# Second layer of a two-layer gated cross-attention kernel: the query projection of groups 3 to 6 as seven block products

## The reference, cut to what matters

```python
def reference(x, ctx, ...):                       # x, ctx: 16 x 64 x 512, float32
    x = x + tanh(g_xattn[0]) * attention_0(layernorm(x), ctx)    # 32 heads of 128, 8 key heads, rotary, mask
    x = x + tanh(g_ffn[0])   * moe(layernorm(x))                 # 16 experts, 2 taken
    x = x + tanh(g_xattn[1]) * attention_1(layernorm(x), ctx)
    x = x + tanh(g_ffn[1])   * lora_moe(layernorm(x))            # 4 experts, 2 taken
    return x

def attention_1(h, ctx):
    q = (h @ Wq.T) -> 32 heads;  k, v = (ctx @ Wk.T), (ctx @ Wv.T) -> 8 heads, each for 4 query heads
    q, k = rmsnorm(q) * q_norm_w, rmsnorm(k) * k_norm_w
    return softmax(q @ k.T / sqrt(128)) @ v -> heads side by side @ Wo.T
```

## Time and profile before

| what | value |
|---|---|
| median of 3 runs | 1178.98 us (1178.72 to 1179.44) |
| profiled execution, its own time | 1179.01 us |
| its span | 1177.1 us |
| TensorE busy | 1169.5 us, 99% |
| VectorE busy | 880.9 us, 75% |
| GpSimd busy | 532.9 us, 45% |
| ScalarE busy | 424.0 us, 36% |
| steps 6 to 13 of layer 2 (866.10 to 1074.70) | 208.60 us |

### The profile page before, as it was taken

One profiled execution on the slowest core, in us unless ns is written; L12 is line 12 of the kernel. 1 busy time (PEld: TensorE's weight loads), 2 busy tenths in 40 slices (PEclk: granted clock), 3 DMA queues, 4 the chain that ended last, 5 costly groups with the idle time before them and its releaser, 6 DMA issues.

```text
span 1177.1 us, 17132 instructions
## 1 busy us (share of the span) xinstructions
PE 1169.5 (99%) x6272; PEld 946.7 (80%) x6272; DVE 880.9 (75%) x1538; ACT 424.0 (36%) x748; POOL 532.9 (45%) x371
## 2 busy tenths in 40 slices
...
PEclk9999999999999999999999999999999999999999
...
DMA packets 57315, 106.54 MB, mean 91 GB/s; under 512 B 3633, under 2 KB 36529, under 8 KB 51889
## 3 DMA queue, kind: packets, MB, share of 16 engines
...
## 4 chain that ended last, share of the span: by engine, by line
PE 96%; DVE 2%; issue 0%; ACT 0%; DVEq 0%; POOL 0%; POOLq 0%
PE ps_q L226 14%; PE ps_b L226 14%; PE ps_b L228 14%; PE ps_b L227 14%; PE ps_q L227 13%; PE ps_q L228 13%; PE ps_s L978 5%; PE ps_b L1005 4%; PE ps_s L278 1%; PE ps_q L953 1%; PE ps_q L2152 1%; PE ps_b L479 1%; PE ps_s L1847 1%; PE ps_q L529 0%; PE ps_b L529 0%
## 5 line engine op out<-in xcount | busy, mean ns | idle before, releaser
L226 PE MATMUL ps_q<-hT_hi,wq_hi 128*128 128x512 f32 x512 | 203.2, 397 | 0.0
L227 PE MATMUL ps_q<-hT_lo,wq_hi 128*128 128x512 f32 x512 | 199.6, 390 | 0.0
L228 PE MATMUL ps_q<-hT_hi,wq_lo 128*128 128x512 f32 x512 | 199.2, 389 | 0.0
L226 PE MATMUL ps_b<-wo_hi,o_hi 128*128 128x512 f32 x440 | 171.6, 390 | 0.0
L227 PE MATMUL ps_b<-wo_lo,o_hi 128*128 128x512 f32 x440 | 171.2, 389 | 0.0
L228 PE MATMUL ps_b<-wo_hi,o_lo 128*128 128x512 f32 x440 | 171.2, 389 | 0.0
L743 POOL TENSOR_TENSOR wq_lo<-wq_raw,wq_hi 128x512 fp32r<-128x512 f32 x64 | 90.2, 1413 | 112.8 <-ACT wq_hi L737 112.8
L1317 POOL TENSOR_TENSOR qT<-q_t 128x512 f32<-128x512 f32 x64 | 89.8, 1405 | 66.3 <-DVE q_t L1430 60.8
L226 PEld LDWEIGHTS ps_q<-hT_hi,wq_hi 128*128 128x128 f32 x512 | 96.1, 188 | 24.3 <-issue 1.5
L228 PEld LDWEIGHTS ps_q<-hT_hi,wq_lo 128*128 128x128 f32 x512 | 96.1, 188 | 20.3
L227 PEld LDWEIGHTS ps_q<-hT_lo,wq_hi 128*128 128x128 f32 x512 | 96.2, 188 | 18.7
...
## 6 DMA issues: line engine op xcount, KB each, us to landing
...
```

The costliest lines, as they stand in the source:

```text
L226: nc.tensor.matmul(dst, l_hi, r_hi, start=first, stop=False)
L227: nc.tensor.matmul(dst, l_hi, r_lo, start=False, stop=False)
L228: return nc.tensor.matmul(dst, l_lo, r_hi, start=False, stop=last)
```

## The change

The weights of a group (512 inputs by 4 heads of 128) and the tokens of a half (512 by 512) are each taken as 2 by 2 blocks. In groups 3 to 6 the four blocks of the query are built from seven products of blocks (Winograd's form) in place of eight. It needs sums of weight blocks (`s1` to `s4`, on GpSimd once a group) and sums of token blocks (`t1` to `t4`, made once for the layer), each split into a high and a low part. A product is 12 matmuls of 256 columns, so a unit has 84 in place of 48 of 512. The results are joined by five adds on VectorE out of PSUM into `qT`, and one copy on ScalarE. The unit's squares are then made from `qT` or the bank in four pieces, and folded by VectorE in two pieces of all four heads (`fold_woven`) in place of four.

The token sums are made with the tiles: ScalarE copies the front tiles' blocks out of the bank (`mixed_front`), VectorE makes t1 and t2 out of the later tiles' banks, GpSimd makes t3 and t4, and the splits follow in steps 2 to 5.

Other edits in layer 2: the eight small copies of the sums move from VectorE to ScalarE in all folded units; TensorE takes the sums of squares ahead of the scores, and waits for the folded squares before the last matmul of the output projection; values wait for the added outputs in two halves; the q and k norm weights are multiplied into the keys; the turned probabilities of units 3 to 13 go into `s_sb` in place of `pT`, which makes the next unit's turned scores wait for `p_lo`; groups 2 and 6 are written out beside the loop; a few semaphore increments are left out; SBUF regions are laid out anew.

```diff
+        def mixed_front(act, i):
+
+            c = lns[2]
+            own, bank = mixed_columns(i), ln_bank(c, i).rearrange("p (k t) -> p k t", k=KC)
+            act.wait_ge(*c("lo", i + 1))
+            nc.scalar.activation(b11_f[:, :, own], bank[:, 0:2, :], ACT.Copy)
+            nc.scalar.activation(b21_f[:, :, own], bank[:, 2:4, :], ACT.Copy).then_inc(att[1]["t_hi"], 1)
...
+            if c is lns[2] and i % PAIRS >= 2:
+                own, bank = mixed_columns(i), ln_bank(c, i).rearrange("p (k t) -> p k t", k=KC)
+                late = i // PAIRS * 2 + i % 2
+                dve.wait_ge(att[1]["t_hi"], late + 1)
+                nc.vector.tensor_tensor(t1_f[:, :, own], bank[:, 0:2, :], b11_f[:, :, own], ALU.subtract).then_inc(att[1]["t_f"], 1)
+                dve.wait_ge(att[1]["t_f"], 2 * late + 1)
+                nc.vector.tensor_tensor(t2_f[:, :, own], bank[:, 2:4, :], t1_f[:, :, own], ALU.subtract).then_inc(att[1]["t_f"], 1)
```

```diff
+        WOVEN_PARTS = ("a11", "s2", "s3", "a12", "s1", "a22", "s4")
...
+        def woven_low(pool, gt, name):
+
+            c = att[1]
+            pool.wait_ge(*c("woven_hi", 7 * (gt - W0) + WOVEN_PARTS.index(name) + 1))
+            f, hi, lo = woven_parts(name)
+            nc.gpsimd.tensor_tensor(lo, f, hi.bitcast(F32), ALU.subtract).then_inc(c["woven_lo"], 1)
+
+        def woven_first_sum(pool, gt):
+
+            s1_f = woven_parts("s1")[0]
+            pool.wait_ge(*att[1]("wq_in", 16 * (gt + 1)))
+            nc.gpsimd.tensor_tensor(s1_f, s1_f, woven_parts("a22")[0], ALU.add).then_inc(att[1]["s_f"], 1)
+
...
+        def woven_last_sum(pool, gt):
+
+            c = att[1]
+            if not (isinstance(gt, int) and gt == W0):
+                pool.wait_ge(*c("q_done", 8 * gt))
+            nc.gpsimd.tensor_tensor(s4_f[:, :, :], woven_parts("a12")[0], s2_f[:, :, :], ALU.subtract).then_inc(c["s_f"], 1)
```

```diff
+            def project_woven(g, h):
+
+                u = 2 * g + h
+                n = u - 2 * W0
+                left = {name: woven_parts(name)[1:] for name in WOVEN_PARTS}
+                tok = [slice(h * HALF + a * QT, h * HALF + (a + 1) * QT) for a in range(2)]
+                own = slice(h * QT, (h + 1) * QT)
+                tokens = lambda rows, a: (hT_hi[:, 2 * rows:2 * rows + 2, tok[a]], hT_lo[:, 2 * rows:2 * rows + 2, tok[a]])
+                mixed = lambda hi, lo: (hi[:, :, own], lo[:, :, own])
+
+                def product(bank, name, right, first, last_one=False):
+
+                    if h == 0:
+                        turn = 7 * (g - W0) + WOVEN_PARTS.index(name) + 1
+                        pe.wait_ge(*c("woven_hi", turn))
+                        pe.wait_ge(*c("woven_lo", turn))
+                    l_hi, l_lo = left[name]
+                    r_hi, r_lo = right
+                    for q in range(2):
+                        for k in range(2):
+                            col = slice(q * D, (q + 1) * D)
+                            dst, closes = bank[:, q * QT:(q + 1) * QT], last_one and (q, k) == (1, 1)
+                            nc.tensor.matmul(dst, l_hi[:, k, col], r_hi[:, k, :], start=first and (q, k) == (0, 0), stop=False, skip_group_check=True)
+                            nc.tensor.matmul(dst, l_hi[:, k, col], r_lo[:, k, :], start=False, stop=False, skip_group_check=True)
+                            last = nc.tensor.matmul(dst, l_lo[:, k, col], r_hi[:, k, :], start=False, stop=closes, skip_group_check=True)
+                    return last
+
+                pe.wait_ge(*c("ssq_t", u))
+                if h == 0:
+                    pe.wait_ge(*c("t_hi", 8))
+                    pe.wait_ge(*c("t_lo", 4))
+                product(ps_q[0], "a11", tokens(0, 0), True).then_inc(c["product"], 1)
+                product(ps_q[1], "s2", mixed(t2_hi, t2_lo), True, True).then_inc(c["product"], 1)
+                pe.wait_ge(*c("s_turned", u))
+                product(ps_h[0], "s3", mixed(t3_hi, t3_lo), True).then_inc(c["product"], 1)
+                pe.wait_ge(*c("copied", n + 1))
+                product(ps_q[0], "a12", tokens(1, 0), False, True).then_inc(c["q_done"], 1)
+                product(ps_h[1], "s1", mixed(t1_hi, t1_lo), True).then_inc(c["q_done"], 1)
+                pe.wait_ge(*c("joined", 5 * n + 2))
+                product(ps_h[0], "a22", mixed(t4_hi, t4_lo), False, True).then_inc(c["q_done"], 1)
+                pe.wait_ge(*c("joined", 5 * n + 3))
+                product(ps_h[1], "s4", tokens(1, 1), False, True).then_inc(c["q_done"], 1)
```

```diff
-                    pe.wait_ge(*c("q_fold", 4 * u + 4))
+                    folded_sums(u, h)
+                else:
+                    pe.wait_ge(*c("q_rot", 4 * u + 4))
...
+            def squares_ready(u):
+
+                pe.wait_ge(*c("q_rot", 4 * u + 4))
+                pe.wait_ge(*c("q_fold", 4 * u + 4))
...
+                    if ahead is not None and j == J - 1:
+                        squares_ready(ahead)
+                    last = nc.tensor.matmul(bank, o_lo[:, t, j, :], hi, start=False, stop=j == J - 1)
```

```diff
+            def fold_woven(u, r):
+
+                own, tok = fold_part(r)
+                other = fold_part(1 - r)[0]
+                dve.wait_ge(*c("q_sq", 4 * u + 2 * r + 2))
+                nc.vector.tensor_tensor(q_sq[own, :, tok], q_sq[own, :, tok], q_sq[other, :, tok], ALU.add).then_inc(c["q_fold"], 2)
```

```diff
+            def woven_step(g, h, next_wq):
+                u = 2 * g + h
+                n = u - 2 * W0
+                building = builds_woven(lay, g, next_wq)
+                if h == 0:
+                    for name in WOVEN_PARTS[4:]:
+                        woven_low(pool, g, name)
+                    for j in range(J):
+                        wo_low(g - 1, j)
+                elif building:
+                    woven_low(pool, g + 1, "a11")
+                att_shift(pool, lay, u - 1)
+                if h and building:
+                    woven_last_sum(pool, g + 1)
+                    woven_low(pool, g + 1, "s2")
+                elif next_wq:
+                    att_wq_low(pool, lay, g + 1, 0)
+                att_normalise(pool, lay, u - 1)
+                if h == 0 and not (isinstance(g, int) and g == G - 2):
+                    woven_first_sum(pool, g + 1)
+                    pool.wait_ge(*c("p_lo", u))
+                    woven_next_sums(pool, g + 1)
+                elif building:
+                    woven_low(pool, g + 1, "s3")
+                    pool.wait_ge(*c("p_lo", u))
+                    woven_low(pool, g + 1, "a12")
+                elif next_wq:
+                    for j in range(1, J):
+                        att_wq_low(pool, lay, g + 1, j)
```

```diff
+            def woven_step(g, h):
+                u, us, up = 2 * g + h, 2 * g + h - 1, 2 * g + h - 2
+                n = u - 2 * W0
+                heads = lambda bank: bank.rearrange("p (j t) -> p j t", j=2)
+                early, late = slice(0, QT), slice(QT, HALF)
+                part_b, part_d = qT[:, h, 0:2, late], qT[:, h, 2:4, late]
+
+                def joined(out, bank, part):
+                    return nc.vector.tensor_tensor(out, heads(bank), part, ALU.add)
+
+                turn_scores(us, 1 - h)
+                scale_scores(us)
+                dve.wait_ge(*c("copied", n + 1))
+                dve.wait_ge(*c("product", 3 * n + 2))
+                joined(part_b, ps_q[1], part_b).then_inc(c["joined"], 1)
+                att_mask(dve, lay, us, 1 - h)
+                dve.wait_ge(*c("joined", 5 * n + 1))
+                dve.wait_ge(*c("product", 3 * n + 3))
+                joined(part_d, ps_h[0], part_b).then_inc(c["joined"], 1)
+                maxima(us)
+                dve.wait_ge(*c("q_done", 4 * u + 2))
+                dve.wait_ge(*c("joined", 5 * n + 2))
+                joined(part_d, ps_h[1], part_d).then_inc(c["joined"], 1)
+                out_low(up, 0)
+                out_low(up, 1)
+                dve.wait_ge(*c("q_done", 4 * u + 3))
+                joined(qT[:, h, 2:4, early], ps_h[0], part_b).then_inc(c["joined"], 1)
+                out_low(up, 2)
+                dve.wait_ge(*c("q_done", 4 * u + 4))
+                joined(part_b, ps_h[1], part_b).then_inc(c["joined"], 1)
+                sums(us)
+                out_low(up, 3)
+                add_output(up, h, 0)
+                turn_probs(us)
+                fold_woven(u, 0)
+                fold_woven(u, 1)
+                att_probs_low(dve, lay, us)
+                add_output(up, h, 1)
+                add_output(up, h, 2)
+                if not (isinstance(g, int) and h):
+                    turn_sums(u, h)
+                add_output(up, h, 3)
```

317 lines of the change are left out of this document (270 added, 47 removed).

## The result

| | before | after |
|---|---|---|
| median, 8 runs each | 1179.20 us (1178.72 to 1179.69) | 1182.28 us (1180.41 to 1183.99, and one of 2347.24) |
| ratio | | 1.0025, 95% interval 1.0015 to 1.0035 |
| profiled execution, span | 1179.01, 1177.1 | 1180.41, 1178.5 |

One execution of the changed kernel took twice the time at a full granted clock; it is a disturbed run and is left out of the ratio. The change made the kernel a little slower: 3 us in the median, but only 1.4 us in the execution that was profiled, the fastest of the eight. Two executions take 1180.4 to 1180.5 with a mean granted clock of 1.000, the five others 1182.0 to 1184.0 with 0.999 to 0.996. A mean of 0.999 by itself says nothing: before's profiled execution has it too, because the clock is at 0.58 in its last 2.1 us (1175.0 to 1177.1), where TensorE has no work left.

The account below looks back on a forecast made before the run. TensorE, with work 99% of the span, was taken as the bound. Its gain of 6.9 us against +1.3 opening, +1.5 even steps, +2.9 step 6 and +0.9 steps 13 and 14 gave -0.3: 1178.7 us, range 1173.0 to 1183.6.

Parts of the forecast that it names:

- Step 6: t4_lo lengthens GpSimd's chain over mask and small maxima; s4 waits 2.8, restart 0.1: +2.9 us (0.5 to 4).
- TensorE's row: 84 matmuls of 256 columns at 0.119 us replace 48 of 512: 0.86 gained a unit, 6.9 over eight units.
- odd step: Steps 7, 9, 11: one GpSimd low, the mask keeps the port, cost 0; about 25.2 us from score to score.
- Rivals 2 and 5: 2: narrow matmuls at 0.106, 1174.7, chance 0.07; 5: they do not cover weight loads, +8.2 a unit, about 1244, chance 0.02.
- Even steps: Steps 8, 10, 12: eight GpSimd lows delay the mask and third add, s4 waits: 0.5 each, +1.5 us.
- P: Start of a step's first projection matmul, 870.18 in step 6, from which the working counts its times in us.
- Steps 13 and 14: VectorE's row longer by 1.2, TensorE's shorter by 0.9, values wait for added outputs: +0.9 us (0 to 1.5).
- The opening: Token sums stand in front of three TensorE waits, in expert network's tail, steps 0 and 2: +1.3 us (0.5 to 2.2).
- Rival 1: The lock costs nothing: VectorE gets the port first at mask and small maxima, s4 waits nowhere; 1174.3 us, chance 0.23.
- Rival 3: Slower: GpSimd gets the port at odd steps' mask and even steps' multiply; up to 1184.8, middle 1183, chance 0.18.
- Rival 4: VectorE's row is the bound, adds, mask and folds losing to GpSimd; gain gone, 1179 to 1182 us, chance 0.08.
- The copies: Eight copies of the sums leave VectorE's woven step, 1.43 us removed there; ScalarE takes them in 1.90.

Follow-up runs that it names:

- e1: The changed kernel again with no edit: median 1182.66 us.
- e4: Changed kernel with GpSimd's last three wq_lo of step 13 made to wait for p_lo: median 1181.15 us.
- e2: Changed kernel with t4's split moved a step earlier, out of GpSimd's row in step 6: median 1179.03 us, ratio to before 0.9999.
- e10: Changed kernel with t4 split earlier and step 13's wq_lo later, plus a long TensorE stall in plain step 5 ahead of its third head: median 1184.09 us.
- e11: Changed kernel with t4 split earlier and step 13's wq_lo later, plus a middle TensorE stall in step 5 ahead of its fourth head: median 1179.63 us.
- e7: Changed kernel with t4 split earlier and step 13's wq_lo later, plus the eight copies of the sums on VectorE again: median 1225.07 us.
- e8: Changed kernel with the plain projection of 48 matmuls in groups 3 to 6, other edits kept: median 1180.38 us, ratio to before 1.0009.

## Why the prediction was wrong

The forecast was 1178.7, within 0.2% of before, range 1173.0 to 1183.6. The measured median, 1182.28, lies in the range, but it is slower than before by 0.26%, with the interval wholly above 1. That it lies in the range is no credit to the sum, which was 3.6 us off. Of these, 1.9 are the median's excess over the profiled execution, and 1.7 are in the profiled execution. The mechanism, a GpSimd row that delays VectorE's third add and so s4, was read rightly. One term was missing, and two waits were mis-sized or put down to the wrong cause.

- **The missing term.** "Step 6: wait +2.8, restart 0.1" priced TensorE's standing still by its length alone. Measured: 3.25 in the profile, and in e1 and e4 a stretch at the lower clock behind the same wait, 1.4 and 2.7 more. The median exceeds the profiled execution, the fastest of its eight, by 1.9: most of it is the clock, as far as is known, and a part, 0.8 at the most, the scatter ahead of step 1. e2 takes out 1.9 of the wait and the slower executions with it; e10 brings the dip about elsewhere, in a trace, and e11 by its times.
- **TensorE's row** was right: 0.118 against 0.119, and an odd step 25.13 against "about 25.2". Rivals 2 and 5 are out. Of the two prices for 256 columns the trace sides with the earlier trace rows; by the Trainium skill (TensorE: Matmul & The Clock Gate, Back-to-back issue gap) it would be 0.109, and the runs do not show that.
- **Even steps**, "0.5 each, +1.5": the mask lost 0.5 as reckoned. The step of the working that failed is that the small maxima are free of GpSimd's row there. The working had GpSimd's lows end at P + 7.6, and its own terms put the start of the small maxima at P + 7.4 to P + 7.6, so nothing kept the two apart. In step 8 (P is 925.03) the lows end at P + 7.9 and the small maxima start at P + 7.3. They lose 0.5 too (1.28), TensorE waits 0.74 and not 0.4, and steps 8, 10 and 12 cost 1.0, 0.9 and 0.8 over an odd one, +2.7 in place of 1.5. The Trainium skill (SBUF — State Buffer, Who interferes with whom) has an exclusive lock there, and counts copies among the instructions that can take it; the rows of steps 6 and 8 and of e7 agree (3.34, 1.28 and 8.19 us in place of 0.78, 0.78 and 1.43).
- **Step 6**: predicted 28, measured 28.6; the wait was 3.25 and not 2.8. The small pieces lost 2.6 and not 2.3, the mask 1.0, and the multiply, which the working had free, 0.4.
- **Steps 13 and 14**, +0.9 because "VectorE's row is longer by 1.2": the place was right and the mechanism wrong. Step 14 is unchanged; step 13 costs 1.5 over an odd one, by GpSimd's three wq_lo beside the folds. That "the folded squares' wait moved to the last matmul of the output projection is met by the same fold" failed there, and the forecast had named this wait among its signs of being wrong. e4 shows it.
- **The opening**, +1.3: 1.1 in the profile, where the scatter ahead of step 1 is in it, and 1.3 by e8's median.
- **The other rivals.** Rival 1 (the lock costs nothing) is out by the mask and the small maxima of steps 6 and 8. Rival 3 has 1183 in its middle, nearer the median than the forecast, but that is luck: the mask of step 7 loses nothing (1.22), the multiply of step 8 neither (1.23), and only step 6's multiply loses 0.4. Rival 4 is out as a bound of every step, since TensorE is busy throughout the odd ones.
- **The copies** were booked as 1.43 less on VectorE and nothing more. By e7, with GpSimd's new row, they are what the whole change hangs on.
- The multiply started at P + 0.8 and not P + 2.0, since the sums of squares now come ahead of the scores; VectorE then waits for the second product, and nothing came of it.

In the profiled execution: 1.1 (opening) + 2.5 (step 6) - 2.8 (7, 9, 11) - 0.1 (8, 10, 12) + 0.6 (13) = +1.3 of the measured +1.4. The forecast's sum, put the same way (each wait less the 0.86 that a step gains), had 1.3 + 2.0 - 2.6 - 1.1 + 0.0, unrounded -0.3. So most of the 1.7 is in the even steps (1.0), step 13 (0.6) and step 6 (0.5), less 0.2 each for the opening and the odd steps.
